# First experts of the audio tower: products issued two pairs at a time, with four sets of activated values

## The reference

```python
gate_logits = x @ gate_w + gate_b
topk_vals, topk_idx = jax.lax.top_k(gate_logits, K)          # K = 2 of E = 16
topk_w = jax.nn.softmax(topk_vals, axis=-1)
h = jax.nn.relu(jnp.einsum('bsh,ehf->bsef', x, w1) + b1)     # 64 -> 128
expert_out = jnp.einsum('bsef,efh->bseh', h, w2) + b2        # 128 -> 64
sel = jnp.take_along_axis(expert_out, topk_idx[:, :, :, None], axis=2)
moe = jnp.sum(topk_w[..., None] * sel, axis=2)
y = x + moe
mu = jnp.mean(y, axis=-1, keepdims=True)
var = jnp.var(y, axis=-1, keepdims=True)
return (y - mu) / jnp.sqrt(var + EPS) * gamma + beta
```

## Time and profile before

| what | value |
|---|---|
| median of 3 runs | 820.14 us (819.86 to 825.51) |
| profiled execution | 823.06 us |
| its span, first to last instruction | 821.1 us |
| mean granted TensorE clock | 0.955 of full speed |
| busy: TensorE, VectorE, ScalarE, GpSimd | 660.8, 616.1, 497.5, 334.4 us |
| first experts, first to last pair on TensorE | 326 to 506 us |
| activations of the experts (line 975) | 128, mean 681 ns |

### The profile page before, as it was taken

How to read it: one execution, slowest core, us unless ns; L and a number is a source line. 1 busy time by engine, 2 the same in 40 slices (tenths; PEclk the granted TensorE clock), 3 DMA queues, 4 the chain that set the end, 5 groups by cost and what they waited for, 6 DMA issues and landing times. The chain is left out here.

```text
span 821.1 us, 16347 instructions
## 1 busy us (share of the span) xinstructions
PE 660.8 (80%) x4968; PEld 371.8 (45%) x4968; DVE 616.1 (75%) x1685; ACT 497.5 (61%) x1246; POOL 334.4 (41%) x410
## 2 busy tenths in 40 slices
PE   0503599999999998999988886475888888889996
PEld 0403266666666665223333222462555555557332
DVE  6678178888888988488889997653788888867653
ACT  2455377776767673466666774533877777763552
POOL 1003156777777786522233332443244444430000
PEclk9999999999999999799999998687999999995999
DMA  4003000000000000343232321000000000000001
GB/s 99 0 9 95 0 1 2 1 0 0 0 0 0 0 0 2 116 170 98 95 93 94 100 93 55 2 0 1 2 1 0 0 0 0 0 2 1 8 20 25
DMA packets 21749, 24.36 MB, mean 30 GB/s; under 512 B 12358, under 2 KB 12614, under 8 KB 21446
## 3 DMA queue, kind: packets, MB, share of 16 engines
q1 hardware_dynamic: 19463, 23.31, 9.3%
q10 hardware_dynamic: 2239, 0.49, 0.3%
HBM read 22.48 MB, written 1.31 MB: 29 GB/s over the span
## 5 line engine op out<-in xcount | busy, mean ns | idle before, releaser
L1309 POOL TENSOR_TENSOR big<-big 128x1024 f32<-128x1024 f32 x64 | 120.5, 1894 | 68.2 <-DVE big L1188 68.2
L1006 ACT ACTIVATE big<-ps,big 128x255 f32<-128x255 f32 x256 | 117.8, 487 | 9.4 <-DVE big L1182 9.3
L975 ACT ACTIVATE big<-ps,b1s 128x512 f32<-128x512 f32 x128 | 80.6, 681 | 39.8 <-PE ps L759 39.7
L1182 DVE TENSOR_REDUCE big<-ps 128x4 f32<-128x1020 f32 x64 | 74.6, 1206 | 32.6 <-PE ps L822 32.6
L1859 DVE TENSOR_REDUCE big<-ps 128x4 f32<-128x1020 f32 x64 | 78.0, 1218 | 11.4 <-PE ps L1500 6.6
L1195 DVE COPY mid<-ps 128x512 f32<-128x512 f32 x128 | 81.9, 680 | 5.5 <-DVE res L1200 2.9
L998 ACT ACTIVATE big<-ps 128x512 f32<-128x512 f32 x64 | 39.5, 618 | 68.2 <-PE ps L810 41.5
L759 PE MATMUL ps<-big,wall 64*128 64x512 f32 x256 | 77.8, 673 | 0.7 <-ACT big L946 0.7
L769 PE MATMUL ps<-big,w2s 128*64 128x512 f32 x256 | 71.5, 638 | 8.0 <-ACT big L975 8.0
L1766 ACT ACTIVATE big<-ps 128x1024 f32<-128x1024 f32 x64 | 65.8, 1029 | 13.6 <-PE ps L1506 9.0
L832 PE MATMUL ps<-cst,big 128*128 128x128 f32 x512 | 71.3, 279 | 2.7 <-DVE mid L1195 1.6
(11 more groups left out here) (265 smaller groups left out, 1365.0 us busy)
## 6 DMA issues: line engine op xcount, KB each, us to landing
mid<-spread_w SPq DMA_DIRECT2D x128, 128.0 KB, 2.8
mid<-in_split_sel SPq DMA_DIRECT2D x1, 1536.0 KB, 7.2
wall<-in_w SPq DMA_DIRECT2D x1, 1280.0 KB, 7.8
out_tokens<-res SPq DMA_DIRECT2D x16, 56.0 KB, 1.6
cst<-in_consts SPq DMA_DIRECT2D x1, 648.5 KB, 7.0
mid<-in_w_raw SPq DMA_DIRECT2D x1, 620.0 KB, 5.6
w2s<-in_w SPq DMA_DIRECT2D x1, 512.0 KB, 3.2
mid<-in_taps ACTq DMA_DIRECT2D x1, 320.0 KB, 3.8
```

What stands on the lines that cost most here:

```text
L975: last = nc.scalar.activation(hid[e % 2][j], H1(e, j), ACT.Relu, bias=b1s[0][:, 2 * e + j:2 * e + j + 1])
L1006: last = nc.scalar.activation(e_sb[r % 4][:, jj, tq, 0:NW], S[:, 2 * (r % 2) + jj, tq, 0:NW], ACT.Exp, scale=-1.0, bias=minus[r % 4][:, jj ...
L1182: nc.vector.tensor_reduce(minus[r % 4], S[:, 2 * a:2 * a + 2, :, 0:NW], AX.X, ALU.min).then_inc(s_mx, 1)
L1309: nc.gpsimd.tensor_tensor(e_sb[r % 4], e_sb[r % 4], bc(inverse[r % 4].unsqueeze(3), [P, 2, 2, 256]), ALU.mult).then_inc(s_A, 1)
```

## The change

On TensorE two first products now stand together, and then two second products: H(e+2), H(e+3), S(e), S(e+1), for e = 0, 2, 4, 6. The small pieces stay behind the same second product as before. One more `hidden`, that of pair 1, stands before the first chunk. The activated values get four sets of tiles instead of two, the two new ones in a part of `big` that was unused at that time; banks of PSUM stay as they are. On ScalarE the wait for `second` now looks four pairs back instead of two, and all its other steps come behind the activation of two pairs later than before (`beside(c, e)` is called when pair s = 8c + e + 2 is activated), but for the copy of the routing weights, which was listed behind e = 6 and is now listed behind e = 5, so behind pair 7. VectorE, GpSimd and SyncE are unchanged.

```diff
-            hid = [[tile(1024 * e + 512 * j) for j in range(2)] for e in range(2)]
+            hid = [[tile((0, 1024, 4352, 5376)[e] + 512 * j) for j in range(2)] for e in range(4)]
...
-                            last = nc.tensor.matmul(Y(e)[D * j:D * j + D], w2s[0][:, 2 * e + j], hid[e % 2][j], start=True, stop=True)
+                            last = nc.tensor.matmul(Y(e)[D * j:D * j + D], w2s[0][:, 2 * e + j], hid[e % 4][j], start=True, stop=True)
...
+                    def after_second(c, q, e):
+                        known = isinstance(c, int)
+                        if e == COLUMNS and (not known or c < CH - 2):
+                            if known and c == 0:
+                                pe.wait_ge(s_O, B)
+                            columns_of(c + 2)
+                        if e == LOGITS and (not known or c < CH - 1):
+                            logits(c + 1, 1 - q)
+                        if e == TURN_SUM and (not known or c >= 1):
+                            sum_turn(c - 1, 1 - q, known and c == CH - 1)
+                        if e == WEIGHTS and (not known or c < CH - 1):
+                            weights(c + 1)
+
                     def duos(c, q):
                         known = isinstance(c, int)
-                        for e in range(DUOS):
+                        for e in range(0, DUOS, 2):
                             s = DUOS * c + e
-                            if e < DUOS - 1:
-                                hidden(q, e + 1, s + 1)
+                            if e < DUOS - 2:
+                                hidden(q, e + 2, s + 2)
+                                hidden(q, e + 3, s + 3)
                             elif not known or c < CH - 1:
                                 pe.wait_ge(s_xc, c + 2)
-                                hidden(1 - q, 0, s + 1)
-                            second(e, s)
...
+                                hidden(1 - q, 0, s + 2)
+                                hidden(1 - q, 1, s + 3)
+                            for n in (e, e + 1):
+                                second(n, DUOS * c + n)
+                                after_second(c, q, n)
...
                     weights(0)
+                    hidden(0, 1, 1)
...
-                    def duos(c, q):
-                        known = isinstance(c, int)
+                    def beside(c, e):
+                        if e == COLUMNS + 1 and c < CH - 2:
+                            columns_out(c + 2, c % 2)
...
+                        if e == GAP and c < CH - 1:
+                            gap(c + 1)
+                        if e in (4, 5) and c >= 1:
+                            own_scale(c - 1, ((0, 1), (2, 3))[e - 4])
+                        if e == WEIGHTS and c < CH - 1:
+                            weights(c + 1, 1 - c % 2)
+
+                    def duos(c):
                         for e in range(DUOS):
                             s = DUOS * c + e
                             act.wait_ge(s_h, s + 1)
-                            if not known or s >= 2:
-                                act.wait_ge(s_w2, s - 1)
+                            if s >= 4:
+                                act.wait_ge(s_w2, s - 3)
                             for j in range(2):
-                                last = nc.scalar.activation(hid[e % 2][j], H1(e, j), ACT.Relu, bias=b1s[0][:, 2 * e + j:2 * e + j + 1])
+                                last = nc.scalar.activation(hid[e % 4][j], H1(e, j), ACT.Relu, bias=b1s[0][:, 2 * e + j:2 * e + j + 1])
                             last.then_inc(s_hid, 1)
...
+                            if s >= 2:
+                                beside((s - 2) // DUOS, (s - 2) % DUOS)
...
+                    for c in range(CH):
+                        duos(c)
+                    for e in (DUOS - 2, DUOS - 1):
+                        beside(CH - 1, e)
```

More of the change, by code:

```diff
@@ L965, in pos_exps @@
                                                  accum_out=psum[:, tq, h:h + 1]).then_inc(s_pexp, 1)
-                    def duos(c, q):
-                        known = isinstance(c, int)
+                    def beside(c, e):
+                        if e == COLUMNS + 1 and c < CH - 2:
+                            columns_out(c + 2, c % 2)
+                        if e in (3, 7) and c >= 1:
+                            for h in (((0,), (1,)) if c == 1 else ((c,), ()))[e // 4]:
+                                pos_exps(h)
+                        if e in (1, 2) and c >= 3:
+                            next_scale(c - 3, ((0, 1), (2, 3))[e - 1])
+                        if e == GAP and c < CH - 1:
[5 more added lines that the diff above has]
+                    def duos(c):
                         for e in range(DUOS):
```

## The result

| what | before | after |
|---|---|---|
| median | 820.00 us (4 runs, 819.54 to 825.51) | 832.16 us (4 runs, 831.45 to 833.74) |
| profiled execution | 823.06 us, span 821.1 | 831.61 us, span 829.7 |
| granted TensorE clock, mean | 0.955 | 0.910 |
| W(0) to the last sum turned, T | 328.69 to 509.47 = 180.78 us | 327.72 to 518.12 = 190.40 us |

The changed kernel is slower: ratio 1.0135, 95% interval 1.009 to 1.0181. The forecast was 832.

A forecast was written before the change was run, and what follows sets the result against it. The loop between TensorE and VectorE, 21.81 us a chunk, was taken as the bound; 1.8 + 7 x 0.49 + 0.4 = +5.7, +12.0 with the clock, on the median 820.14 gives 832 us; range 824 to 840.

The forecast's parts named there:

- What bounds the loop: Each chunk is a loop of two legs between TensorE and VectorE, 9.44 + 12.37 = 21.81 us.
- From S(2) to W: Leg from pair 2's second product to the transposes of the next chunk's routing weights; stays 9.44 us, set by VectorE's chain.
- The rival at 809: VectorE's backlog is the bound, so both TensorE stalls go, 7 x 1.57 = 11 us less; chance 0.07.
- One H more in the second leg: Routing-weight transposes to next chunk's pair 2 second product: six first products instead of five, 1.06 us a chunk without saving.
- the saving in bursts: Adjacent like products pay start and end once: two first products 1.92 us, two second 1.87; growth +0.49 a chunk.
- The rival without saving: Each weight load waits for the product before it, 7 x 0.57 + 0.4 more, 836 to 837 us; chance 0.20.
- the 0.85: Streaming time in us of one second product at full clock, worked out as 2 x 512 columns; it takes 1.01.
- Four sets and ScalarE's later steps: TensorE's 1.11 us stall before pair 5's second product goes, but the gain is worth nothing; later ScalarE steps cost 0.
- The wait before W: TensorE's idle time before the routing weights' transposes: 3.8 us in one piece, instead of 2.1 in two.
- The clock: TensorE's clock falls around the routing weights' transposes six times instead of two: 4 x 1.55 = +6.3 us.
- The rival at 826: The loop grows but the clock keeps its present falls or fewer, 826 down to 823 us; chance 0.19.
- The start: Two more first products before the first chunk's pair 2 second product, partly at the lower clock: +1.8 us.

The follow-up runs named there:

- 4: Changed kernel with VectorE's search for the indices moved from behind pair 2 to behind pair 1; 825.50 us, ratio 1.0052 to the kernel before.
- experiment 5: Kernel before with VectorE's search for the indices moved from behind pair 2 to behind pair 1; 815.62 us, ratio 0.9944.
- experiment 3: Changed kernel with three unused matmuls ahead of the routing weights' transposes in six chunks; 825.96 us, ratio 1.006 to the kernel before.
- experiment 1: Kernel before, its product order kept, with four sets of activated values and ScalarE's scalings and exponentials two activations later; 826.27 us, ratio 1.0064.
- experiment 2: Changed kernel with two sets of activated values instead of four, and ScalarE's old wait; 833.55 us, ratio 1.0151 to the kernel before.
- experiment 7: Kernel before with experiment 1's edits, the indices behind pair 1 and GpSimd's position scores at the chunk's start; 804.98 us, ratio 0.9821.
- experiment 8: Changed kernel with only GpSimd's position scores moved to the start of the chunk; 831.44 us, ratio 1.0137 to the kernel before.
- 6: Changed kernel with the turning of the routing weights one pair later, behind the second product of pair 6; 851.56 us, ratio 1.0397 to the kernel before.
- experiment 10: Kernel before, two sets and old ScalarE order kept, with indices behind pair 1 and position scores at the chunk's start; 807.59 us, ratio 0.9841.

## Why the prediction was right

- *What bounds the loop.* Right. From S(2) to W 9.44 was forecast and is 9.44. Shortening that leg alone sped up both orders (4, 5); VectorE was not the bound by its backlog, since its idle time before the weighing of pair 2 grew from 1.07 to 1.93 (1.5 to 2.1 forecast). The rival at 809 fell. One reading was off: the seven waits are not one for each chunk after the first. One of 0.94 stands before the very first W, none before the second (348.29), and six of 0.97 or 0.98 before the others. The forecast of six falls isn't touched by it.
- *One H more in the second leg, and the saving in bursts.* Right: H H 1.92 and S S 1.87, as forecast, the leg 12.93 against 12.86, so +0.56 a chunk against +0.49 (experiment 3). Behind the last W it is +0.86 (27.58 against 26.72), again as forecast. The rival without saving fell: it needs H H in 2.12. The working behind the 0.85 doesn't come out as written: 2 x 512 columns at 2.4 GHz are 0.43. But the second H or S of a burst adds 0.86 (1.92 - 1.06 and 1.87 - 1.01), so 0.85 was the right size, and it takes two periods of the clock for each of these columns. The rule of the Trainium skill ("TensorE: Matmul & The Clock Gate", Part 3, "The mechanism"), that a weight load overlaps running matmuls only in another row group, doesn't describe these bursts; the measurement decides. The same section also lets a load go ahead when its target is the background weight buffer; the saving would fit that, and no run here tells whether it is the cause.
- *Four sets and ScalarE's later steps.* Right that they are worth nothing in the loop of the old order: 21.81 in experiment 1 with a wait of 2.15 before W, where 2.1 was forecast. Its profiled execution has three clear falls of the clock behind W where that of before has two; one execution of each can't show that the longer wait brought the third. In the new order the four sets are worth 0.6 a chunk (experiment 2), which the prediction didn't price.
- *The wait before W.* 3.48 by its row for 3.8 forecast. The leg is the same, so TensorE ended later in it: S(4) S(5) lasts 2.17 where S(2) S(3) lasts 1.94, by a gap before S(5), and the rest lies in the modelled ends.
- *The clock.* Six falls were forecast: behind the six waits of 3.48 there are six, five inside periods 3 to 7 and one behind the last W; period 2, whose wait was 1.77, has 0.69 over fall-free, where before had 0.55. The price was 1.65 instead of 1.55 (4 x 1.55 is 6.2, where the sum has 6.3). In the six periods from the second the excess over fall-free is 8.95 after (over 22.37) and 3.60 before (over 21.81): +5.35, and +3.36 for the loop (6 x 0.56) makes the +8.71. Experiment 3 shows it by taking the idle stretch away: no fall behind six filled waits, periods of 22.37. The rival at 826 held for the loop and fell for the clock.
- *The start.* Wrong in sign in the comparison as made, +1.8 forecast and -1.41 seen. The row it was worked out from, 340.77, belongs to an execution with a long stretch at the low clock (granted clock 0.80 from 320 to 345 us, where after and experiment 1 have 0.93): the first period of before was 19.60, that of experiment 1, with the same order of products, 17.09. Against that the change's 18.19 is +1.1. So the step of the start failed twice: 1.8 was too much for its two H, and a single execution's slow start was taken as the kernel's.
- *The sum.* +12.0 was forecast against the profile's own execution, which would have become 835; it became 831.6. Of the 3.4 between them 0.97 lies ahead of W(0), where nothing was edited. The stage grew by 9.62, 2.4 short of the sum: 3.2 from the start (+1.8 against -1.4), less 0.8 elsewhere. The medians differ by 12.16, as forecast to 0.2, but that closeness is partly luck: the executions of before that weren't profiled were mostly 3 us below the profiled one, and no profile shows where.

**What stays open.** From T to the end profiled executions took 311.5 to 312.2 us in eight kernels and 316.3 to 319.0 in four (experiments 1, 3, 7 and 8), in code that no edit touched. The mean granted clock over it was 0.91 in the eight and 0.89 in the four. All twelve have a long stretch at the low clock late in it (749 to 766 in after); the four fell once more ahead of it, about 223 us behind T, and experiment 3 stayed low longer. Whether this follows from when the stage begins or is chance wasn't tried. It puts up to 7 us into a comparison of totals, so experiments 1, 3 and 8 are read by their stages. Open too are the long or second falls of the clock that some chunks of experiments 2, 4, 6, 7 and 8 have.

## What to carry to other kernels

Before work is regrouped, write the loop as legs between the points where the engines hand over; a regrouping that left the waiting leg as it was and added a product to the other one lost, and the gain lay in shortening the leg (here the indices and the position scores moved: 1.6% in experiment 10, 1.8% in 7). Gathering small stalls into one long one isn't neutral on TensorE: in this kernel two pieces of 1 us brought a fall in two chunks of six, one of 3.5 in six of six, and a fall cost 1.65. Compare stages from landmark to landmark over several kernels, since one profile's start, or its last 300 us, can carry several microseconds of clock that have nothing to do with the edit.

## What the runs showed of the hardware

- The fall of the clock can show after the idle stretch that goes before it: 1.00 in the two windows from 368 to 370, 0.56 and 0.50 in the next two, with TensorE idle up to 368.97. The array then pays for it in busy work: H H in 3.27 instead of 1.92. It isn't always so: before the last sum of the kernel before, idle for 3.71 up to 509.47, the window from 508 to 509 is already at 0.63.
- A few matmuls nobody needs, 2.84 us of them, kept the clock: no fall behind six filled waits in the profiled execution of experiment 3.
- VectorE's small operations are held up by GpSimd's large ones. In after, of the eight operations of line 1113 one is four times as long as most, 1244 ns, beside a GpSimd addition of 1.26 that starts inside them, and one is twice as long, 0.60, beside the scaling before it. By source (columns: count, then min/median/max in ns) of after and of experiment 7; then one row of VectorE and two of GpSimd from the timelines of after:

```profile
L1113 DVE TENSOR_SCALAR big<-cst,big x8: 281/290/1244, 389.7 to 392.4; 128x16 f32<-128x16 f32 x8
```

```profile
L1106 DVE TENSOR_SCALAR big<-cst,big x8: 288/292/297, 406.7 to 408.1; 128x16 f32<-128x16 f32 x8
```

```profile
389.93 0.60 DVE L1113 TENSOR_SCALAR big<-cst,big 128x16 f32<-128x16 f32 x1
```

```profile
389.78 0.72 POOL L1295 TENSOR_SCALAR pexp<-big 128x512 f32<-128x512 f32 x1
390.58 1.26 POOL L1296 TENSOR_TENSOR pexp<-pexp,big 128x512 f32<-128x512 f32 x1
```

  Moved to the start of the chunk, the same instruction held up an addition of 128 x 512 there instead (1.17, where the others take 0.68), in a place where VectorE had more time (experiment 7, VectorE and GpSimd):

```profile
417.69 1.17 DVE L1148 TENSOR_TENSOR big<-big 128x512 f32<-128x512 f32 x1
```

```profile
417.04 1.27 POOL L1289 TENSOR_TENSOR pexp<-pexp,big 128x512 f32<-128x512 f32 x1
```

  The Trainium skill has this as a pair of ports that VectorE and GpSimd share, held for a whole instruction while the other blocks ("SBUF — State Buffer", "Terms"). The trace agrees: the long operation ends at 391.87 and GpSimd's addition of 1.26 at 391.84, and the one of 0.60 ends at 390.53, with the scaling (390.50). GpSimd's first scaling does the same to VectorE's product of 128 x 4, in after (0.34, to 389.70, the scaling to 389.68) and in experiment 5 (0.64). Together the hold-ups take 1.4 us of the leg in after: the product from 0.16 to 0.34 and the eight operations from 1.68 to 2.94 (experiment 8 and after).
